# A decoder layer on one core: a new merge of two tiles' steps and a new set of fill matmuls

## The reference

```
1 gated delta rule, 16 heads of 16: a rotating recurrence gives cond; q, k, v from hidden @ ctrl_W + cond @ delta_W,
  causal convolution of 4 taps, silu, l2norm; then over time
     S = g * S;  S = S + k (beta * (v - k S));  o = q S
  rmsnorm(o) * silu(gate) @ out_proj
2 cross attention to the 64 context tokens, 32 half heads of 8: softmax(q1 k1) v - lam * softmax(q2 k2) v, rmsnorm, @ Wp
3 depthwise causal convolution of 3 taps, silu; router takes 2 of 8 experts, all 8 are computed (silu(x1 @ expert_w)),
  weighted and summed; @ out_w; rmsnorm; gelu feed forward of 64
```

## Time and profile before

| | us |
|---|---|
| median of 3 runs | 1768.73 (1756.36, 1768.73, 1771.37) |
| the profiled execution's own time | 1769.48 |
| its span, first to last instruction | 1767.7 |
| PE busy | 1606.6 (91%) |
| DVE busy | 1253.4 (71%) |
| ACT busy | 862.6 (49%) |
| POOL busy | 222.4 (13%) |
| mean granted TensorE clock | 0.97 |

### The profile page before, as it was taken

The page is one execution under the profiler, slowest core; times in us unless marked ns, Lnnn a source line. Parts: engine busy times, 40 slices in busy tenths (PEclk is TensorE's granted clock), DMA queues, the critical chain, the costliest instruction groups (busy, mean ns, idle before and its releaser), DMA issues.

```text
span 1767.7 us, 40617 instructions
## 1 busy us (share of the span) xinstructions
PE 1606.6 (91%) x17030; PEld 1115.6 (63%) x17096; DVE 1253.4 (71%) x3201; ACT 862.6 (49%) x1626; POOL 222.4 (13%) x212
## 2 busy tenths in 40 slices
PE   5868999989999999999999999999999999999888
PEld 2456667576665667566675666656666666756664
DVE  6575677865887668876788658885688766787554
ACT  2731376433844348443664337543484435744343
POOL 0121003010121002120030101210021200301000
PEclk9975999999999999999999999999999999999899
DMA  5000001000010001000000000100010000100000
GB/s 210 24 14 2 13 13 26 2 26 1 13 25 3 25 1 37 2 3 24 13 25 2 14 13 12 25 3 26 1 35 4 3 12 1 37 2 14 1 1 12
DMA packets 20221, 31.81 MB, mean 18 GB/s; under 512 B 1480, under 2 KB 17864, under 8 KB 19784
## 3 DMA queue, kind: packets, MB, share of 16 engines
q1 hardware_dynamic: 20040, 29.22, 5.4%
HBM read 20.81 MB, written 8.39 MB: 17 GB/s over the span
## 4 chain that ended last, share of the span: by engine, by line
PE 62%; DVE 17%; ACT 15%; issue 6%; POOL 1%; DVEq 0%; ACTq 0%; POOLq 0%
PE bank L1737 12%; PE bank L1691 5%; PE bank L1667 4%; PE bank L1677 3%; PE four L1462 3%; PE bank L1360 3%; PE bank L1385 3%; PE four L1532 3%; PE four L1398 2%; PE four L1584 2%; PE four L1600 2%; PE four L1551 2%; PE bank L1398 2%; ACT L553 2%; PE bank L1392 2%
## 5 line engine op out<-in xcount | busy, mean ns | idle before, releaser
L1737 PE MATMUL bank<-w_sb,cs 128*128 128x512 f32 x512 | 258.8, 612 | 0.5
L789 ACT ACTIVATE cs<-bank 128x512 f32<-128x512 f32 x128 | 75.8, 592 | 184.7 <-remote 122.5
L745 ACT COPY cs<-bank 128x512 f32<-128x512 f32 x128 | 74.8, 585 | 157.6 <-PE bank L1677 157.6
L690 ACT ACTIVATE qkv<-mk,c_sb 128x256 f32<-128x256 f32 x256 | 107.9, 497 | 70.9 <-PE four L1551 68.4
L1310 DVE SCALAR_TENSOR_TENSOR cs<-cs,rwt 128x256 f32<-128x256 f32 x224 | 121.6, 543 | 17.2 <-ACT cs L789 10.9
L1691 PE MATMUL bank<-vx_sb,cs 128*128 128x136 f32 x1024 | 132.5, 282 | 0.0
L1691 PEld LDWEIGHTS bank<-vx_sb,cs 128*128 128x128 f32 x1024 | 126.9, 191 | 7.3 <-issue 6.7
L518 POOL TENSOR_TENSOR decayed<-state,pk 128x512 f32<-128x512 f32 x64 | 70.8, 1106 | 475.7 <-DVE state L1146 475.7
L1737 PEld LDWEIGHTS bank<-w_sb,cs 128*128 128x128 f32 x512 | 87.9, 189 | 66.0 <-issue 54.7
L1462 PE MATMUL four<-hT,w_sb 128*128 128x512 f32 x256 | 126.1, 616 | 1.4 <-DVE rotb L1002 1.3
L1398 PEld LDWEIGHTS four<-c_sb 128*128 128x128 f32 x784 | 104.5, 200 | 36.0 <-issue 23.3
(11 more groups left out here) (242 smaller groups left out, 3203.0 us busy)
## 6 DMA issues: line engine op xcount, KB each, us to landing
xt<-in_x SPq DMA_DIRECT2D x8, 512.0 KB, 3.8
...
```

The lines of the kernel that those rows point to most:

```text
L690: last = A(mkq[:, c % 2, :, h, :], src, ACT.Copy, scale=C("q4")[:, h:h + 1])
L789: fin("moe_act", A(ye[:, u % 4, :], bank[5 + u % 3][:, :], ACT.Silu))
L1737: mm(dst, x1T[:, k, b * TB:b * TB + TB], ew[:, k, ep * 512:ep * 512 + 512], start=k == 0, stop=False)
```

## The change

Two tables get new numbers; no step's own code changes, the order inside each half stays, and no step is added or removed. The number of fills in a joint tile goes from 98 to 86. What the new `BESIDE` does to the queues, read from the merged lists ("A | B" is before | after):

- PE, front of the tile: `gate.0` stands between `pt.0` and `pt.1` (before: after `pt.2`); `unrot` after `pt.4`; `turn1` ahead of `qx.1`; `proj.0 pt.6 proj.1 pt.7 pv.3 sc.5 pt.8 db pt.9 proj.2 pv.4 sc.6 pt.10 proj.3 pt.11 pv.5 sc.7 pt.12 pt.13` | `proj.0 pt.6 proj.1 pt.7 db pv.3 sc.5 pt.8 pt.9 pv.4 sc.6 pt.10 proj.2 pt.11 pv.5 sc.7 pt.12 proj.3 pt.13`.
- PE, middle: `raw.0..3 turn4.0 turn3.1 wp.1 pw.0 raw.4..7 turn4.1 router.0 moe.0 moe.1 pw.1` | `raw.0 raw.1 turn4.0 raw.2 raw.3 turn3.1 wp.1 pw.0 raw.4 raw.5 turn4.1 raw.6 router.0 raw.7 moe.0 moe.1 d1.0 pw.1`. Ahead of `z.0` stand `moe.0` to `moe.18` | `moe.17`.
- PE, end: `turn5.0 cs.0.0` | `cs.0.0 moe.19 cs.0.1 turn5.0`; `mi z.6` | `z.6 mi`; `turn6.0 d1.5` | `d1.5 turn6.0`.
- DVE: `max.0 max.1 rot` | `max.0 rot max.1`; `av.6 conv.2` | `conv.2 av.6`; `wp.0 gsub norm.1` | `gsub norm.1 wp.0`; `anorm.1 am.0` | `am.0 anorm.1`; `am.2 am.3 dconv.1 solve.0` | `am.2 x1T.0 dconv.1 am.3 solve.0`; `acc.0` to `acc.5` | `acc.4` ahead of `solve.15`; `acc.15 zc.6 m.4 hnorm.0 o.3 s.4` | `zc.6 acc.15 m.4 o.3 s.4 hnorm.0`.
- ACT: `pt.12 pt.13 max.7 spread blog` | `pt.12 proj.3 pt.13 spread blog max.7`; `db` and `proj.2` behind `max.6`; `kx.0 ln3.0 kx.1` | `kx.0 kx.1 ln3.0`. On POOL `ffd.0` stands behind `dec.6`.
- Fills, places with the larger differences: `tinv` 1, 1, 1, 2, 7 at 0, 1, 3, 4, 6 | 2, 2, 2, 2, 1, 1, 1 at 0 to 4, 6, 7; `pv.7` 5 | 1; `sum.1` 4 | 1; `turn5.1` 5 | 1; `router.0` 5 | 3; `turn6.0` 2 | 6; `sc.0.0` 1 | 4; `qx.0` 1 | 3; `raw.4` and `pw.0` 2 | 0 each.

```diff
@@ -134,11 +134,11 @@
     moe.28 moe.29 moe.30 moe.31 mi acc.14 acc.15 hnorm.0 turn5.1 turn6.0 mo.1 hnorm.1 ffd.0 turn6.1 ffu.0 ffd.1 ffu.1''')
 
 
-KEEP = {("turn1",): 7, ("rot",): 1, ("unrot",): 1, ("raw", 0): 4, ("raw", 4): 2, ("tinv", 0): 1, ("tinv", 1): 1,
-        ("tinv", 3): 1, ("tinv", 4): 2, ("tinv", 6): 7, ("onorm",): 2, ("wo",): 11, ("turn2", 0): 11, ("qx", 0): 1,
-        ("sc", 0, 0): 1, ("pt", 0): 2, ("pv", 6): 1, ("pv", 7): 5, ("turn3", 1): 9, ("turn4", 0): 1, ("turn4", 1): 1,
-        ("pw", 0): 2, ("router", 0): 5, ("turn5", 1): 5, ("turn6", 0): 2, ("turn6", 1): 2, ("ffu", 1): 1,
-        ("proj", 0): 4, ("sum", 0): 1, ("sum", 1): 4}
+KEEP = {("turn1",): 7, ("unrot",): 2, ("cond",): 1, ("raw", 0): 5, ("raw", 7): 1, ("tinv", 0): 2, ("tinv", 1): 2,
+        ("tinv", 2): 2, ("tinv", 3): 2, ("tinv", 4): 1, ("tinv", 6): 1, ("tinv", 7): 1, ("onorm",): 1, ("wo",): 11,
+        ("turn2", 0): 12, ("qx", 0): 3, ("sc", 0, 0): 4, ("pt", 0): 1, ("pt", 10): 1, ("pv", 7): 1, ("turn3", 1): 8,
+        ("turn4", 0): 2, ("router", 0): 3, ("turn5", 1): 1, ("turn6", 0): 6, ("ffu", 1): 1, ("proj", 0): 3,
+        ("sum", 1): 1}
 
 
 def kept(steps):
@@ -149,16 +149,16 @@
 FIRST, SECOND = kept(FIRST), kept(SECOND)
 
 
-BESIDE = {"pe": [0, 0, 1, 1, 1, 1, 1, 1, 2, 4, 4, 4, 4, 4, 4, 4, 4, 4, 7, 7, 7, 7, 7, 8, 8, 9, 9, 11, 12, 12, 12, 12, 12,
-                 13, 14, 14, 14, 14, 15, 15, 15, 15, 15, 15, 19, 19, 19, 20, 23, 24, 26, 27, 27, 33, 33, 33, 34, 34, 34, 34,
-                 38, 38, 38, 38, 38, 38, 38, 38, 38, 38, 38, 39, 39, 40, 40, 40, 41, 41, 41, 41, 41, 41, 41, 41, 45, 46, 48,
-                 49, 51, 52, 54, 55, 56, 56, 61, 62, 63, 66, 66, 67, 69, 72, 74, 74, 78, 80, 82, 83, 85, 89, 91, 93],
-          "dve": [0, 0, 2, 2, 3, 3, 3, 4, 5, 5, 6, 6, 6, 6, 7, 7, 7, 10, 13, 17, 17, 17, 18, 18, 18, 19, 21, 28, 35, 38, 38,
-                  39, 44, 44, 46, 51, 53, 56, 58, 60, 61, 64, 66, 66, 68, 70, 76, 84, 84],
-          "act": [0, 0, 0, 0, 1, 2, 2, 2, 2, 2, 2, 2, 3, 3, 4, 5, 5, 5, 5, 6, 6, 6, 8, 9, 9, 10, 10, 10, 10, 19, 21, 23, 29,
-                  35, 35, 35, 37, 37, 38, 38, 38, 38, 38, 39, 39, 39, 39, 39, 39, 39, 40, 40, 40, 40, 40, 40, 40, 40, 41,
-                  41, 42, 42, 42, 43, 43, 44, 44, 44, 44, 44, 44, 46, 46, 46, 46, 46, 46, 46, 46, 46, 46],
-          "pool": [23, 25]}
+BESIDE = {"pe": [0, 0, 1, 1, 1, 1, 1, 2, 2, 3, 3, 3, 3, 4, 4, 5, 5, 5, 5, 5, 5, 5, 5, 7, 8, 9, 10, 11, 12, 13, 13, 13, 13,
+                 13, 13, 13, 13, 13, 13, 14, 14, 14, 14, 14, 15, 19, 19, 21, 22, 23, 25, 25, 25, 30, 32, 32, 32, 32, 34, 35,
+                 35, 37, 37, 39, 40, 40, 40, 40, 41, 42, 42, 42, 43, 43, 43, 43, 43, 45, 45, 45, 45, 46, 48, 49, 49, 50, 52,
+                 55, 56, 57, 58, 60, 62, 63, 66, 67, 67, 69, 71, 72, 74, 76, 79, 81, 84, 86, 90, 92, 94],
+          "dve": [0, 0, 2, 3, 3, 3, 3, 4, 5, 5, 5, 5, 6, 6, 6, 7, 7, 11, 15, 17, 17, 18, 18, 19, 19, 20, 20, 29, 38, 40, 41,
+                  42, 45, 50, 51, 53, 53, 54, 54, 59, 62, 62, 66, 67, 69, 72, 76, 83, 84],
+          "act": [0, 0, 0, 0, 1, 2, 2, 2, 3, 3, 3, 3, 3, 3, 4, 5, 5, 7, 7, 7, 7, 7, 7, 7, 7, 7, 9, 10, 12, 18, 21, 22, 30,
+                  35, 35, 35, 37, 37, 38, 38, 38, 38, 38, 38, 38, 39, 39, 39, 39, 39, 39, 39, 39, 39, 39, 39, 39, 39, 40,
+                  40, 42, 42, 42, 43, 43, 43, 43, 43, 43, 45, 45, 46, 46, 46, 46, 46, 46, 46, 46, 46, 46],
+          "pool": [25, 25]}
 
 
 def merged(engine, first, second):
```

## The result

| | before | after |
|---|---|---|
| median, us | 1768.49 | **1772.82** |
| lowest to highest of 20 runs each | 1756.36 to 1771.42 | 1766.15 to 1778.97 |
| ratio, after to before | | 1.0037, 95% interval 1.0022 to 1.0052 |
| profiled span | 1767.7 | 1770.5 |

The change does not make the kernel faster: it is slower by 0.2 to 0.5%, which is within 1%. I had forecast 1745.

What follows compares the result with a forecast made beforehand. The bound was taken to change along a tile: PE, ACT, DVE, then the loop PE-DVE-PE. Six items summed to -4.0 us a tile, taken as -2.7, times seven -19; with clock -5, 1769.5 became 1745 us, range 1727 to 1771.

Steps and rivals of the forecast that it cites:

- Item 1: Attention at the tile's front, PE-bound: more fills and the parted sc.4 cost, turn1 and proj.2 gain; +0.3 us a tile.
- Item 2: ACT's stretch of silu and norms: blog runs in the wait ahead of max.7, norm.1's wait goes; -1.3 us a tile.
- Item 3: From raw to solve: am.0 fills a DVE wait, fewer fills, turn4.1 and dconv.1 earlier; -1.6 us a tile.
- Item 4: The solve, DVE-bound: one acc (0.93 us) fewer stands ahead of z.0; -0.9 us a tile.
- Item 5: The recurrence, where PE is full: one expert pair moved there from ahead of z.0; +1.0 us a tile.
- Item 6: End of the recurrence: zc.6 and z.6 earlier, hnorm.0 out of the way, turn6.0's fills under o.3; -1.5 us a tile.
- clock: Half-clock stretches after db and in the recurrence, costing 9.4 us: half of that saved, -5 us for the whole kernel.
- rival B: Fills gone ahead of z.0 leave PE idle, a further clock drop of 1.56 us a joint tile; 1761 us; chance 0.10.
- clock rule: The skill lays half clock to idle time between matmul bursts; the prediction held the trace against it, PE being busy in drops.
- Rival C: In the attention, DVE's rot delays max.1, so PE waits at sc.2.0, up to 2.9 us a tile; 1790 us; chance 0.13.
- Rival A: Waits are conserved, each place won opening the next; the merge gains nothing, only the clock 5 to 9; 1760-1765; chance 0.22.

Runs made afterwards that it cites:

- e4: Changed kernel with the three fills of proj.0 moved behind sc.4.1, so sc.4.0 and sc.4.1 run side by side; 1762.36 us, ratio 0.9991 to the kernel before.
- e12: Changed kernel with 8 fills ahead of vturn, sc.4 halves together, and the first third in the old order with old fills; 1751.28 us.
- e9: Changed kernel with 8 fills ahead of vturn, sc.4 halves together, and max.7 ahead of spread and blog on ACT again; 1753.47 us.
- e7: Changed kernel with 8 fills ahead of vturn, sc.4 halves together, and old PE turn4.0 to moe.1 and DVE am.0 to dconv.1; 1761.10 us.
- e11: Changed kernel with 8 fills ahead of vturn, sc.4 halves together, and DVE's old order from solve.0 to solve.15; 1770.58 us.
- e14: Kernel before with the new DVE order from solve.0 to solve.15 and without the 9 fills of tinv.4 and tinv.6; 1754.22 us, ratio 0.9939.
- e13: e12 with moe.18 on PE ahead of z.0 again; 1751.87 us, ratio 0.9927 to the kernel before.
- e10: Changed kernel with 8 fills ahead of vturn, sc.4 halves together, and the recurrence's end in old order and fills; 1759.57 us.
- e1: Changed kernel with 8 fills more, ahead of vturn; 1759.36 us, ratio 0.9959 to the kernel before.
- e15: Changed kernel with the old fills at sum.1 (4) and pv.7 (5) put back and none at vturn; 1769.38 us, ratio 1.0020 to the kernel before.
- e2: Changed kernel's new BESIDE merge with the old KEEP table of fills; 1791.67 us, ratio 1.0139 to the kernel before.

## Why the prediction was wrong

| term, us a tile | predicted | in the two traces | undone or mended alone |
|---|---|---|---|
| 1 front | +0.3 | +1.13 | 0.75 (e4) and 0.4 to 0.5 (e12) |
| 2 ACT's stretch | -1.3 | +0.42 | 0.0 (`blog` alone, e9) |
| 3 `raw` to `solve` | -1.6 | -0.80 | 0.5 (e7) |
| 4 solve | -0.9 | -1.69 | 2.4 (e11), 2.0 at `tinv` (e14) |
| 5 one step more in the recurrence | +1.0 | +0.83 | not undone (e13 only moves a wait) |
| 6 end of the recurrence | -1.5 | -0.30 | 0.4 (e10) |
| sum (taken) | -4.0 (-2.7) | -0.41 | |
| clock, whole kernel | -5 | +7.5 | -17 (e1) |

**The step that failed most is the clock:** -5 forecast, +7.5 measured, 12.5 us off; with its wait covered the time is 1759 (e1). The merge is 16 us off over seven tiles (-19 against -3); the largest term in it is item 2, 12 us off (-1.3 against +0.42 a tile). I weighed the clock by the places where the kernel before drops, and judged those rightly: `db` and the recurrence are mended (no half clock there in any joint tile of the profiled execution). But I never went through the waits that the new table leaves open. The order on PE has `pv.7` ahead of `sum.3` now; that opens 2.16 us ahead of `vturn`, of which the seven fills that went at `sum.1` and `pv.7` explain 0.63 (e15). e1 shows that covering this one wait is worth 13 us in the medians (1772.82 to 1759.36) and 16.8 in the seven periods of the profiles. My rival B had the mechanism, a wait without cover and narrow matmuls behind it, but at `z.0`, where nothing dropped: there the wait after the expert pairs is 0.6 us and no fills are missed. Its price of 1.56 for each was right for the short stretches only; the long ones cost 5.6 to 5.9.

On the clock rule I argued too far. The earlier trace rows show that a drop can come in busy PE; from that I held that idle time mattered little. The Trainium skill ("TensorE: Matmul & The Clock Gate", section "A second HAM failure mode: psum-queue depth-cycling") describes a clock that falls when PE idles briefly but often between groups of matmuls. The changed kernel, e15 and e1 agree with it, with 2.16, 1.53 and 0 us of idle time and six, six and no tiles with half clock; e2 does not, with 1.80 us and none. I also took 1756.36 for a run with eight fewer drops; the profile has six in joint tiles, and the last tile alone can differ by more than 6 us.

**Item 2 failed at its premise.** ACT's queue does set `silu.0`, but the wait of 0.74 into which I put `blog` was filled by another step of the same change, the emptying of `proj.3`, which I had counted on PE alone. On ACT it waits 1.86 for its matmuls, and `proj.2` and `db` were moved behind `max.6` as well; I did not price these three. More than half of the +0.42 is no matter of ACT at all: 0.10 of it is there at `silu.0`, 0.19 at `vturn`, and the last 0.23, between `vturn` and `raw.0`, is the fifth fill of `raw.0`, which stands behind PE's wait of 0.76 and so on the path, where I had held that fills count nothing. The 0.61 of `norm.1` did not go either; ACT waits for DVE at the same place in the changed kernel:

```profile
896.13 0.69 ACT L545 ACTIVATE mk<-four,small 128x512 f32<-128x512 f32 x1 [0.61 <-DVE kq L1043]
```

**Item 1** had the right mechanism for `sc.4` and charged 0.5 for what cost 0.75. In the first third the 0.6 that I charged for more fills at `qx.0` and `sc.0.0` is there (`sc.0.0` starts 0.59 later); the 0.8 that I credited for `turn1` and `proj.2` is not: `cond` is 0.53 late, and from `proj.0` to `conv.0` 0.14 comes back. Rival C did not come: `sc.2.0` does not wait for DVE. It is DVE that waits, 1.75 us for PE's `rot`, at the head of `max.1` (timeline of DVE, after; the row answers to the earlier trace rows):

```profile
819.50 0.69 DVE L983 TENSOR_TENSOR rota<-four,cosT 128x512 f32<-128x512 f32 x1 [1.75 <-PE four L1360]
```

**Item 3** was right in sign and two to three times too large in size (1.6 against 0.8 in the traces and 0.5 undone alone): I moved `dconv.1` at its old duration into a stretch where POOL works, and `raw.7` behind `router.0` comes 2.2 us later.

**Item 4** was right and too small. I counted the one `acc` (0.93) and did not look at `top`, which moved one and a half steps back; in the old place DVE waits for ACT's exponential there. `z.0` follows directly on `tinv`, as I had said (944.49, the transposes end at 944.39), though PE was ready only 0.63 us ahead and not 2.

**Item 5** was right: +1.0 forecast, +0.83 measured, and the traces show the step in a stretch that PE fills. **Item 6** gains 0.3 to 0.4 and not 1.5: the 1.2 at `z.6` came, but the 6 fills of `turn6.0`, which I had put under `o.3`, hold `z.7` for 1.4 us after it, and `hnorm.0` only moved from ahead of `o.3` to ahead of `zc.7`.

Rival A, each place won opens a wait at the next, is near to what the merge turned out to be: 0.41 us a tile. It gave 1760 to 1765, which is close to the merge with its clock mended (e1: 1759), but its clock had the wrong sign.
